# Four score banks, joint score bursts and a new placement of stages in a cross-attention, self-attention and expert kernel

## What is computed

```
x = x + xattn(layernorm(x), ctx)      # 16 heads of 32, keys = values = ctx; softmax over 257; @ W_out.T + b
x = x + attn(layernorm(x))            # low-rank q and kv projections, rope, 16 heads, softmax over 32; @ Wo + b
x = x + ffn(layernorm(x))             # 8 experts, top 1: gelu(x @ W1 + b1) @ W2 + b2
```

## Time and profile before

| what | value |
|---|---|
| median of three runs | 910.48 us (908.25 to 910.67) |
| the profiled execution: own time | 908.74 us |
| its span, first to last instruction | 906.5 us |
| PE busy | 790.9 us (87%) |
| DVE, ACT, POOL busy | 562.7, 402.0, 317.9 us |
| mean granted TensorE clock | 0.959 of full speed |
| start, to the scores of batch 4 (weights are prepared) | 0 to 73.5 us |
| tiles 1 to 15 | 73.5 to 649 us |
| rest of the stages of the last tiles | 649 to 713.5 us |
| routing | 713.5 to 729.7 us |
| experts | 729.7 to 906.5 us |

### The profile page before, as it was taken

How to read it: one execution, slowest core, us unless ns; L and a number is a source line. 1 busy time by engine, 2 the same in 40 slices (tenths; PEclk the granted TensorE clock), 3 DMA queues, 4 the chain that set the end, 5 groups by cost and what they waited for, 6 DMA issues and landing times.

```text
span 906.5 us, 26770 instructions
## 1 busy us (share of the span) xinstructions
PE 790.9 (87%) x10852; PEld 596.3 (66%) x10852; DVE 562.7 (62%) x1191; ACT 402.0 (44%) x1019; POOL 317.9 (35%) x661
## 2 busy tenths in 40 slices
PE   4896879899898998989989899898885289999998
PEld 2444657667676676767767677676774167777775
DVE  3467576776767767777676776767633543555552
ACT  2343364554645546455464645545313133333332
POOL 1112343332433324233242323323310245566652
PEclk9898999999999999999999999999976589999999
DMA  9854454545545445455454444443230398433320
GB/s 272 275 116 95 123 136 111 148 107 134 137 106 147 112 119 144 114 137 123 108 148 122 122 136 109 133 127 84 82 117 12 121 336 325 121 104 98 102 84 3
DMA packets 109705, 118.94 MB, mean 131 GB/s; under 512 B 13326, under 2 KB 80142, under 8 KB 109584
## 3 DMA queue, kind: packets, MB, share of 16 engines
q1 hardware_dynamic: 103680, 105.15, 43.0%
q0 software_dynamic: 3680, 10.23, 3.4%
q10 hardware_dynamic: 2224, 1.86, 0.7%
HBM read 108.82 MB, written 10.22 MB: 131 GB/s over the span
## 4 chain that ended last, share of the span: by engine, by line
PE 70%; DVE 11%; ACT 6%; issue 5%; POOL 3%; SPq 3%; DMA 2%; POOLq 0%; DVEq 0%
PE bank L440 10%; PE scores L1357 9%; PE bank L1372 9%; PE bank L441 8%; PE bank L442 8%; PE scores L471 5%; PE bank L484 4%; PE bank L434 3%; PE bank L498 3%; DVE negmax L924 2%; DMA keys<-in_ctx 2%; PE bank L642 2%; POOL operand_lo L1162 2%; PE bank L558 2%; ACT prob L727 2%
## 5 line engine op out<-in xcount | busy, mean ns | idle before, releaser
L727 ACT ACTIVATE prob<-scores,negmax 128x257 f32<-128x257 f32 x256 | 119.3, 472 | 178.4 <-DVE negmax L924 170.4
L924 DVE TENSOR_REDUCE negmax<-scores 128x2 f32<-128x514 f32 x128 | 87.8, 686 | 48.4 <-PE scores L471 48.3
L914 DVE STREAM_TRANSPOSE k_t<-keys 128x512 f32<-128x512 f32 x128 | 90.4, 707 | 42.8 <-DMA keys<-in_ctx 42.5
L1141 POOL COPY plast<-prob 128x2 f32<-128x2 f32 x128 | 24.1, 188 | 225.7 <-ACT prob L727 225.7
L440 PE MATMUL bank<-qkv_hi,operand_hi 128*128 128x396 f32 x256 | 98.7, 386 | 0.4 <-DVE operand_lo L928 0.4
L1357 PEld LDWEIGHTS scores<-rows_t,w 128*128 128x128 f32 x736 | 87.8, 196 | 11.6 <-issue 10.5
L471 PE MATMUL scores<-k_t,q_t 32*32 32x257 f32 x2048 | 86.7, 395 | 6.8 <-ACT q_t L688 4.0
L441 PE MATMUL bank<-qkv_lo,operand_hi 128*128 128x396 f32 x256 | 88.8, 347 | 0.0
L1357 PE MATMUL scores<-rows_t,w 128*128 128x128 f32 x736 | 88.1, 279 | 0.7 <-ACT rows_t L1395 0.7
L442 PE MATMUL bank<-qkv_hi,operand_lo 128*128 128x396 f32 x256 | 88.4, 345 | 0.0
L498 PEld LDWEIGHTS bank<-prob_t,context 128*32 128x32 f32 x4096 | 47.4, 112 | 56.0 <-DVE prob_t L919 30.8
(11 more groups left out here) (218 smaller groups left out, 1604.3 us busy)
## 6 DMA issues: line engine op xcount, KB each, us to landing
keys<-in_ctx SPq DMA_DIRECT2D x256, 128.0 KB, 4.4
context<-in_ctx SPq DMA_DIRECT2D x64, 512.0 KB, 4.4
w_all<-in_L_ffn_W SPq DMA_DIRECT2D x16, 1024.0 KB, 10.8
b<-in_L_ffn_b SPq DMA_DIRECT2D x23, 256.0 KB, 3.5
x_tile<-in_x SPq DMA_DIRECT2D x8, 256.0 KB, 4.7
x_pair<-in_x SPq DMA_DIRECT2D x8, 256.0 KB, 4.8
x_scratch<-x_tile SPq DMA_DIRECT2D x8, 256.0 KB, 2.0
x_scratch<-x_pair SPq DMA_DIRECT2D x8, 256.0 KB, 2.0
```

The costliest lines, as they stand in the source:

```text
L727: act.activation(prob[pair][:, gg, :], scores[:, gg, 0:J], ACT.Exp, bias=negmax[b % 2][:, g:g + 1], accum_out=sums[t % 2][:, g, bl:bl + 1] ...
L914: dve.transpose(dst, src).then_inc(keys_turned, 1)
L924: dve.tensor_reduce(negmax[b % 2][:, 2 * pair:2 * pair + 2], scores[:, :, 0:J], AX.X, ALU.max, negate=True).then_inc(maxed, 1)
```

## The change

What it does:

- `scores` has four banks, one for each head group; the stages have three banks instead of four, and `prob_bank` is gone. T of a pair writes into the first bank of that pair's own scores, once its exponentials are done. S of a pair in the next batch waits for that pair's move (`prob_moved`), and no longer for exponentials.
- Both S of a batch are issued together, at step 0. The two maxima stand together at step 2, then the four exponentials. T stands at steps 6 and 8, A at 10 and 12, keys at 5 and 7, `keep_last` and `move_last` at 7 and 9. ACT moves pair 0 and DVE pair 1.
- `bank_of` is new, and nearly every stage has a new place.
- The two low-rank biases are still loaded at step 0; the other nine small DMAs are issued at step 8, and POOL's use of them is a step of its own, 24. POOL's sum at step 6 now has no `keep_last` ahead of it in its step.

Cut to its core:

```diff
-    -4, -1, -5, 0, 0, 5, 3, 5, 5, 5, 11, 15, 16, 20, 23, 19, 40, 40, 47, 47, 48, 51, 54, 57, 55, 60, 82, 87, 91, 96, 110, 120, 122, -46)
-MEASURE_X, SCALE_X = 2 * STEPS + 2, 2 * STEPS + 14
+    -5, 0, -5, -6, 3, 3, 3, 4, 4, 2, 10, 17, 19, 21, 24, 26, 41, 41, 45, 46, 46, 50, 48, 56, 55, 63, 83, 89, 86, 95, 105, 105, 118, -54)
+MEASURE_X, SCALE_X = 2 * STEPS + 4, 2 * STEPS + 5
...
-SCORE_AT = (0, 5)
-KEYS_AT = (1, 6)
-TURN_P_AT = (5, 10)
-ATTEND_AT = (8, 16)
-KEEP_AT = (0, 6)
-DVE_PROB = (0,)
+SCORE_AT = (0, 0)
+MAX_AT = (2, 2)
+KEYS_AT = (5, 7)
+TURN_P_AT = (6, 8)
+ATTEND_AT = (10, 12)
+KEEP_AT = (7, 9)
+DVE_PROB = (1,)
...
-UNIT_AT = (2, 4, 5, 6, 8, 9, 10, 11, 12, 13, 14, 15, 16, 17, 19, 24, 27, 29, 30, 33, 34, 35, 37, 38, 39)
+UNIT_AT = (2, 3, 5, 6, 7, 8, 9, 10, 11, 13, 14, 15, 17, 19, 22, 23, 26, 28, 29, 31, 32, 33, 36, 37, 38)
...
-ROT_K_AT = 18
+ROT_K_AT = 20
+SUM_AT = 6
+TURN_ROT_K_AT = 12
+BIAS_LOAD_AT = 8
+BIAS_TURN_AT = 24
...
-    scores = ctx.enter_context(nc.psum_tensor("scores", [P, 2, 512], F32))
-    psum = [ctx.enter_context(nc.psum_tensor(f"bank{i}", [P, 512], F32)) for i in range(6)]
-    prob_bank, att_bank, banks = psum[0], psum[1], psum[2:6]
+    scores = ctx.enter_context(nc.psum_tensor("scores", [P, G, 512], F32))
+    psum = [ctx.enter_context(nc.psum_tensor(f"bank{i}", [P, 512], F32)) for i in range(4)]
+    att_bank, banks = psum[0], psum[1:4]
...
-    bank_of = {"queries": 1, "spread": 1, "xout": 0, "norm": 2, "qkv0": 2, "qkv2": 0, "out": 0, "inv": 2, "gate": 1, "av": 3, "qkv1": 3, "q": 3, "k": 2, "norm3": 3, "rank": 1, "qkv3": 2, "self": 3}
+    bank_of = {"queries": 0, "spread": 0, "xout": 0, "norm": 1, "qkv0": 1, "qkv2": 1, "out": 2, "inv": 1, "gate": 0, "av": 0, "qkv1": 2, "q": 1, "k": 0, "norm3": 1, "rank": 0, "qkv3": 0, "self": 1}
...
-            until.wait_ge(exped, 4 * b + 2 * pair)
+            until.wait_ge(prob_moved[pair], b)
...
         def turn_prob(b, pair):
             until.wait_ge(exped, 4 * b + 2 * pair + 2)
-            if pair == 0:
-                until.wait_ge(prob_moved[1], b)
-            else:
-                until.wait_ge(prob_moved[0], b + 1)
...
-                    done = pe.transpose(prob_bank[:, at:at + P], prob[pair][:, gg, c * P:(c + 1) * P], ident)
+                    done = pe.transpose(scores[:, 2 * pair, at:at + P], prob[pair][:, gg, c * P:(c + 1) * P], ident)
...
             if step == 0:
+                load_low()
+            if step == BIAS_LOAD_AT:
                 load_small()
```

More of the change, by code:

```diff
@@ L334, in program @@
                "out": x2_made, "norm3": x3_moved, "gate": gate_used, "rank": rank_used}
+    last_bank = banks[(bank_of["queries"] + 1) % 3]
+    units_of_bank = [[n for n, at in enumerate(UNIT_AT) if n % 3 == bank_of["queries"] and (at > TILE + TILE + QUERIES) == after] for after in (False, True)]
     def emptied_stage(stage, t):
@@ L445, in bank_for @@
             before = bank_before(stage, t)
-            if before is None:
+            if stage == "queries" and t == 1:
+                for n in units_of_bank[0]:
+                    until.wait_ge(*emptied_unit(n))
+            elif t == 0:
                 until.wait_ge(bias_moved, 4)
                 until.wait_ge(weight_lo, CUTS.index(("v", G - 1)) + 1)
-            else:
+            if before is not None:
                 until.wait_ge(*emptied_stage(*before))
@@ L470, in score @@
                     rows, place = slice(hl * HD, (hl + 1) * HD), hl ^ (2 * pair + gg)
-                    done = pe.matmul(scores[place * S:(place + 1) * S, gg, 0:J], q_t[rows, 2 * pair + gg, bl, :],
+                    done = pe.matmul(scores[place * S:(place + 1) * S, 2 * pair + gg, 0:J], q_t[rows, 2 * pair + gg, bl, :],
                                      k_t[pair][rows, gg, :], start=True, stop=True)
@@ L660, in tensor_program @@
             b, k = divmod(step, STEPS)
-            if k == SCORE_AT[0] and b < B:
-                score(b, 0)
+            for pair in range(2):
+                if k == SCORE_AT[pair] and b < B:
+                    score(b, pair)
             if k == ATTEND_AT[1] - STEPS and 1 <= b <= B:
                 attend(b - 1, 1)
-            if k == SCORE_AT[1] and b < B:
-                score(b, 1)
             if k == TURN_P_AT[0] and b < B:
@@ L716, in move_prob @@
             until.wait_ge(attended, 2 * b - 1 + pair)
-            act.activation(prob_t[pair][:, :, :, :].rearrange("p g c n -> p (g c n)"), prob_bank[:, :], ACT.Copy).then_inc(prob_moved[pair], 1)
+            act.activation(prob_t[pair][:, :, :, :].rearrange("p g c n -> p (g c n)"), scores[:, 2 * pair, :], ACT.Copy).then_inc(prob_moved[pair], 1)
         def exp(b, g):
@@ L726, in exp @@
                 until.wait_ge(inverted, t - 1)
-            act.activation(prob[pair][:, gg, :], scores[:, gg, 0:J], ACT.Exp, bias=negmax[b % 2][:, g:g + 1],
+            act.activation(prob[pair][:, gg, :], scores[:, g, 0:J], ACT.Exp, bias=negmax[b % 2][:, g:g + 1],
                            accum_out=sums[t % 2][:, g, bl:bl + 1]).then_inc(exped, 1)
@@ L815, in scalar_program @@
         until.wait_ge(last_turned, 1)
-        act.activation(last_t[:, :, :].rearrange("p g b -> p (g b)"), banks[2][:, 0:G * B], ACT.Copy).then_inc(last_ready, 1)
+        act.activation(last_t[:, :, :].rearrange("p g b -> p (g b)"), last_bank[:, 0:G * B], ACT.Copy).then_inc(last_ready, 1)
         for step in range(LAST_STEP):
             b, k = divmod(step, STEPS)
-            if k == SCORE_AT[0] and b < B:
+            if k == MAX_AT[0] and b < B:
                 exp(b, 0)
@@ L918, in move_prob @@
             until.wait_ge(attended, 2 * b - 1 + pair)
[L919 removed]
+            dve.tensor_copy(prob_t[pair][:, :, :, :].rearrange("p g c n -> p (g c n)"), scores[:, 2 * pair, :]).then_inc(prob_moved[pair], 1)
         def largest(b, pair):
@@ L1075, in vector_program @@
                 turn_keys(b + 1, 0)
-            if k == SCORE_AT[1] and b < B:
+            if k == MAX_AT[1] and b < B:
                 largest(b, 1)
@@ L1339, in turn_rows @@
         def turn_rows(s):
-            bank = (prob_bank, att_bank)[s % 2]
+            bank = (scores[:, 2, :], att_bank)[s % 2]
             until.wait_ge(normed_e, s + 1)
```

34 lines of the change are left out of this document (20 added, 14 removed).

## The result

| | before | after |
|---|---|---|
| median of four runs, us | 909.47 (908.25 to 910.67) | 878.03 (876.87 to 880.12) |
| profiled execution, us | 908.74 | 876.87 |
| its span, us | 906.5 | 874.6 |
| PE busy in the span | 87% | 87% |

The ratio is 0.9657, 95% interval 0.9632 to 0.9682: the change takes 31 us away.

What follows compares the result with a forecast made beforehand. The prediction took PE, busy 87% of the span, to bound the kernel. Gains of 11.2 us (middle), 1.0 (start) and 1.7 (end), together 13.9, took 908.74 to 895 us, range 882 to 906.

Steps and rivals of the forecast that it cites:

- Joint S: Middle tiles: issuing both score bursts together hides 0.1 us a batch, bound 0.3, so 0.4 a tile.
- Four tenths of a us fewer waits a tile: Middle tiles: PE's idle time falls from 3.17 to 2.8 us a tile, 0.4 saved.
- the walk: One middle tile followed in the new order, each operation placed after its last need, giving 2.8 us of PE idle time.
- the waits only change their names: Rival, middle: idle stays 3.17 us a tile and joint S hides nothing; 906 us, chance 0.10.
- The keys: Middle tiles: key loads get 7 us more time, so DVE's 2.4 us wait for keys ends.
- S behind `move_last`, new, 0.6: Middle tiles: the next scores wait 0.6 us for `move_last`, behind POOL's softmax scaling; a new wait.
- The start, 1.0, bounds +3 and -4: Start: POOL's sum begins 2.7 us earlier, of which 1.0 us is kept as gain, bounds +3 and -4.
- The rival of equal turns: Rival, start: without early DMA traffic sharing equally, weights land 3.8 us earlier; 891 us, chance 0.04.
- The end, 1.7: After the last batch: gate of tile 14 runs ahead of av, so out starts 1.7 us earlier, bounds 0 and 3.
- The sum: Whole kernel: 11.2 us from 14 middle tiles, 1.0 from the start and 1.7 from the end, 13.9 us saved.
- a time near 874: Rival, middle: waits mostly vanish, idle falls to 1.5 us and 2.3 us a tile is saved; 874 us, chance 0.10.
- My three signs of being wrong: A tile over 38 us, S waiting over 1 us on POOL, or batch 4's scores coming later than before.

Runs made afterwards that it cites:

- the start as before: Kernel after, with ACT issuing all eleven small DMAs at step 0 and POOL keeping batch 0's last probabilities ahead of its sum: 876.69 us.
- the early last keys: Kernel after, with POOL keeping the last probabilities and placing the last keys at step 2 instead of steps 7 and 9: 871.9 us.
- the alternating pairs: On top of the early last keys, a batch's 32 score matmuls issued alternately from pair 0 and pair 1: 870.68 us.

## Why the prediction was wrong, step by step

- *Joint S, 0.1 a batch, bound 0.3.* This is the step that failed. The array gains 0.45 to 0.47 a batch, and undoing it costs 1.18 a tile and 18 us in all, where the sum had 5.6. I bounded it by "up to half a burst" of the pair that comes second, and then took 0.1 as nearest to a change of shape. The runs show two parts, 0.16 for neighbours and 0.29 for free places. The joint scores also work in tiles 0 and 1, which my 14 tiles left out.
- *Four tenths of a us fewer waits a tile.* Right in size, in part by luck: with the scores apart, a tile took 37.73 against 38.11, 0.38, but that is 0.61 of idle time less and 0.21 of busy time more, which the walk did not have. The parts were right in name and mostly in size: inv 0.6 forecast and 0.74 (0.5 with the scores apart), norm3 0.4 and 0.59, xout 0.5 and 0.51, S 0.6 and 0.32, gate 0.4 and 0.34, norm 0.2 and 0.29. One I had not seen: qkv waits 0.3 for DVE's low part. The idle time stayed at 3.15 only because 0.59 of the burst's gain turned into waiting. So the rival "the waits only change their names" was right in its words and wrong in its price, as it had joint S hide nothing.
- *The keys.* I booked the end of DVE's 2.4 us as a gain within the walk and named the load. The turn's place matters for another reason, DVE's order: at the old steps it stands ahead of x2 and the maxima, and the tile is some 3 us longer. No run shows what the end of the 2.4 us is worth by itself.
- *S behind `move_last`, new, 0.6.* Seen at 0.32 and proven by taking it away: 0.46 a tile.
- *The start, 1.0, bounds +3 and -4.* Its mechanism stands in the rows: in both profiles of the kernel after the sum starts when its weights have landed (18.23 and 20.00), in the kernel before it started at 22.30 and 22.50. The forecast gap of 1 us ahead of rot didn't come, as the nine DMAs took 5.4 us of ACT (24.51 to 29.9) and not 7. But none of it can be found at batch 8: with sum and q units 2.8 later than in the first profile nothing was lost there, so that the term can't be told from 0. The rival of equal turns would have had the weights land 3.8 us earlier without the broadcasts. Their load took 8.2 and 10.0 us with the nine late, and 9.6, 8.3, 8.7 and 10.5 with all eleven early: no difference that stands out of the scatter. By the Trainium skill (DMA: Bandwidth & Descriptors, "Queues, rings and completion order") each DMA engine takes turns between the queues that have work; these loads don't show it at the size that equal shares of the bytes would give.
- *The end, 1.7.* Right where I looked: out is 1.70 nearer to av. The whole end gained 3 to 5.9 by the four profiles. Of the 5.6 between the first two, 2.3 lie between the first scores of batch 60 and av of tile 15 (692.99 - 611.85 = 81.14, against 664.38 - 585.58 = 78.80), where the joint scores of four batches are at work, 1.7 are out, and 1.6 stand behind out, which I had left as it was. The four profiles of kernels with the order of the kernel after there (the kernel itself twice, the nine DMAs at step 0, the start as before) scatter from 285.57 to 289.02.
- *The sum.* With joint S at its measured 18 in the place of 5.6, the same sum gives 13.9 + 12.4 = 26, and 882. The 4 or 5 us that remain lie ahead of batch 8, where the change gained about 5 and the start's order nothing that can be seen, and in the end. Tile 1 is 3 us shorter in both profiles (39.69 and 40.00 against 42.92 and 43.34), of which joint scores are up to 2 (41.70 without them); what the rest is I haven't settled, and the scatter of single executions there is as large.
- *The chances.* I gave 0.10 to a time near 874, but for a reason that didn't happen, idle time of 1.5 a tile. The idle time never fell. My three signs of being wrong didn't come true (a tile of 36.55, S waiting 0.32 on POOL, the scores of batch 4 at 70.73 against 73.48): all three looked for a slower kernel, and none for a burst cheaper than my bound.

## What to carry to other kernels

Price a burst of small matmuls by the places of the array that it uses, not by its length alone: two bursts on different places run in one another, and here 64 such pairs made the larger part of the gain. Then ask which chain PE waits for behind it, since a third of what PE saved (0.59 of 1.70 us a tile) came back as waiting. And when a wait looks cheap to remove, look at where its idle time goes: banks of their own for inv and gate removed the waits they were made for, gathered the rest in one place and came out 7 us slower, with a clock that fell in five of thirteen tiles, while the edit that took a late helper off a wait (two small copies on POOL) gave 6 us. The quickest kernel of this study has the change, the early last keys and the alternating pairs: 870.68 us, 4.3% under the kernel before.

## What the runs showed of the hardware that I had not expected

- fp32 matmuls of 32 x 32 with 257 columns: 16 of them hold the array for 0.59 us to the next matmul; 32 on sixteen places 0.73, 32 with the pairs alternating 0.68, 32 on eight places 1.02.
- 1.85 us of idle PE within 3.3 us, around few matmuls, was followed in four tiles by a stretch of 3 us at a mean clock of 0.53 to 0.60 (most of it at the lower level, 1.2 GHz), in a fifth by a longer fall, and in eight tiles with the same waits by none. With the idle time spread over the tile, as in the kernel after, the clock stood at 1.00 in 25 of the 26 middle tiles of two profiles.
- One 512 KB load at the start of the kernel, issued at 9.95 to 9.97 us in six profiles, took between 8.2 and 10.5 us to land, whether nine broadcast loads ran beside it or not. In the two profiles of the kernel after it took 8.2 and 10.0, and the scores of batch 8 stood 3.3 us apart.
